# Output products as three float16 terms on 64x64 tiles, y in two float16 parts, and the dynamic convolution in far and near parts

## The reference

```python
xn = group_norm(x, 32 groups)
f = relu(Wc @ xn + bc)                          # 64 channels
gk1 = relu(mean(xn) @ Wc.T + bc)                # pixel mean
g_kern = gk1 * Wkk + bkk                        # 3x3 per channel
sk = relu(Wc @ max over 16x16 blocks of xn + bc)  # 3x3 per channel
dynW = relu(Wck[:, 0] * g_kern + Wck[:, 1] * sk + bck)   # 64x64x3x3 of each image
y = conv3x3(f, dynW) + b_ad
out = x + Wf @ y + bf                           # back to 256 channels
```

## Time and profile before

| what | us |
|---|---|
| median of three timed runs | 511.08 |
| lowest and highest of them | 510.58, 513.79 |
| span of the profiled execution, first to last instruction | 507.5 |
| median less span | 3.6 |
| PE busy in the span | 487.8 (96%) |
| ACT, DVE, POOL busy | 426.6, 418.9, 296.2 |
| DMA, mean rate over the span | 311 GB/s |

### The profile page before, as it was taken

The page is one execution under the profiler, slowest core; times in us unless marked ns, Lnnn a source line. Parts: engine busy times, 40 slices in busy tenths (PEclk is TensorE's granted clock), DMA queues, the critical chain, the costliest instruction groups (busy, mean ns, idle before and its releaser), DMA issues.

```text
span 507.5 us, 19231 instructions
## 1 busy us (share of the span) xinstructions
PE 487.8 (96%) x8349; PEld 383.7 (76%) x8349; DVE 418.9 (83%) x653; ACT 426.6 (84%) x486; POOL 296.2 (58%) x231
## 2 busy tenths in 40 slices
PE   5989999999999999999999999999999999999993
PEld 2454664677788888888888978888887878888781
DVE  6978879988888889888888988888889887888544
ACT  5779999998999999999999899999999989995231
POOL 5224586555577655556775555577655556765543
PEclk9999999999999999999999999999999999999997
DMA  8945778999898998998999999989999998953467
GB/s 335 418 134 201 265 283 289 366 353 349 323 333 334 323 332 340 348 359 293 320 362 333 333 365 343 318 297 360 307 366 334 341 333 298 361 208 145 185 270 296
DMA packets 48868, 158.01 MB, mean 311 GB/s; under 512 B 4752, under 2 KB 15888, under 8 KB 48784
## 3 DMA queue, kind: packets, MB, share of 16 engines
q1 hardware_dynamic: 34096, 93.07, 54.0%
q10 hardware_dynamic: 14688, 63.70, 31.0%
HBM read 75.94 MB, written 75.50 MB: 298 GB/s over the span
## 4 chain that ended last, share of the span: by engine, by line
PE 81%; ACT 2%; DVE 0%; issue 0%; DVEq 0%; ACTq 0%
PE ps L1129 30%; PE ps L1260 23%; PE ps L1228 21%; PE ps L1179 7%; ACT unused L609 1%; DVE X L859 0%; ACT unused L596 0%; ACT f_hi L688 0%; DVEq L153 0%; ACT f L694 0%; ACT Y L586 0%; PE ps L1372 0%; ACT dyn_b L709 0%; ACT dyn_hi L707 0%; ACTq L130 0%
## 5 line engine op out<-in xcount | busy, mean ns | idle before, releaser
L859 DVE SCALAR_TENSOR_TENSOR X<-ps,out_bias,X 128x960 f32<-128x960 f32 (+1 forms) x189 | 185.2, 1008 | 17.1 <-PE ps L1260 16.8
L1260 PE MATMUL ps<-Y,const 64*64 64x480 f32 (+1 forms) x1536 | 165.1, 486 | 0.0
L596 ACT ACTIVATE unused<-X,neg_mean 128x2304 bf16<-128x2304 f32 x60 | 132.0, 2201 | 0.4 <-DVE neg_mean L998 0.4
L512 POOL TENSOR_TENSOR dyn_a<-const,pool_g 128x576 f32<-128x576 f32 x30 | 34.9, 1165 | 163.8 <-DVE pool_g L883 163.8
L609 ACT ACTIVATE unused<-X 128x2304 bf16<-128x2304 f32 x60 | 126.9, 2115 | 0.0
L1228 PE MATMUL ps<-X,wcn_t 64*64 64x384 f32 (+1 forms) x1296 | 115.5, 486 | 0.7 <-issue 0.7
L935 DVE TENSOR_REDUCE feats<-X 128x6 f32<-128x1536 f32 x64 | 111.6, 1744 | 0.0
L1228 PEld LDWEIGHTS ps<-X,wcn_t 64*64 64x64 f32 x1296 | 82.0, 133 | 29.8 <-issue 7.4
L1260 PEld LDWEIGHTS ps<-Y,const 64*64 64x64 f32 x1536 | 78.2, 133 | 7.5 <-issue 2.8
L527 POOL TENSOR_TENSOR f_lo<-f,f_hi 128x1152 f16<-128x1152 f32 x32 | 71.4, 2232 | 19.5 <-ACT f L694 19.5
L1129 PE MATMUL ps<-f_hi,dyn_hi 64*64 64x480 f16 x1152 | 69.0, 365 | 2.5 <-ACT dyn_hi L715 1.1
(11 more groups left out here) (101 smaller groups left out, 541.8 us busy)
## 6 DMA issues: line engine op xcount, KB each, us to landing
X<-x SPq DMA_DIRECT2D x63, 1152.0 KB, 9.5
out<-X ACTq DMA_DIRECT2D x54, 1152.0 KB, 9.7
out<-X SPq DMA_DIRECT2D x7, 1152.0 KB, 8.0
out<-X SPq DMA_DIRECT2D x6, 480.0 KB, 3.5
stack<-f_hi SPq DMA_DIRECT2D x64, 32.5 KB, 2.5
stack<-f_lo SPq DMA_DIRECT2D x64, 32.5 KB, 5.4
X<-x SPq DMA_DIRECT2D x2, 576.0 KB, 7.1
upper<-f_hi SPq DMA_DIRECT2D x32, 32.5 KB, 3.5
```

Of the source, the lines that this page charges most:

```text
L596: nc.scalar.activation(unused[:, t], pixels(u, t), ACT.Square, scale=1.0 / SIDE, bias=neg_mean[:, n % 2, 1:2], accum_out=feats[:, (n + 1) ...
L859: nc.vector.scalar_tensor_tensor(out=out, in0=unit_psum(piece, bank, col), scalar=out_bias[:, t:t + 1], in1=out, op0=ALU.add, op1=ALU.add) ...
L1260: mm = nc.tensor.matmul(ps[rows, bank + q, col:col + width], wft[lanes, t, rows], Y[lanes, n % 2, at:at + width], start=True, stop=True)
```

## The change

- Output units: wft is scaled by a power of two and split into float16 parts wf_hi and wf_lo (wf_small is wf_hi over 4096). y is split into Y_hi and Y_lo (float16). Each unit is now three products in place of one float32 product. There are four units of 336 columns and two of the near part; the near units run as `products_near`, 12 groups of 4 matmuls of 240 columns, whose row tiles exchange the PSUM bank halfway. Y_hi and Y_lo have one buffer each.
- Convolution: in place of main and rest, a far part (7 rows of each tile, 336 columns) and a near part (5 rows, 240 columns), each with three terms of 9 groups of 4 matmuls. The near part reads one row across the middle of the image, which SP copies (four copies of 64x52 elements for each image in place of five of 64x260). `stack`, `upper` and `conv_rest` are gone.
- y leaves PSUM in four instructions: ACT writes Y_hi of the far part and of the near part (`y_high_out`), DVE writes Y_lo of each (`y_low_out`).
- Output bias: `channel_mean` on ACT now adds it to x in place while it sums (for images 0 and 1 POOL does it, `add_bias`). DVE's maxima wait for that.
- ACT no longer makes the relu of the dynamic weights; POOL does, with two-operation TENSOR_SCALARs (min with a large number, then max with 0). POOL's first product is now TENSOR_SCALAR on a stored per_gain, and POOL also makes the Newton factor. ACT takes over f_bias and mean_act from DVE.
- The projection is cut 512, 512 and 128 (+11) columns, with a new order of turns. Squares are now taken of image i+3. SP issues all stores.
- New orders on every engine, and new orders for the first four and last two images.

Core of the diff (lines left out are marked):

```diff
-CONV_BANKS = (0, 1)
-REST_BANK = 6
+ROWS = (7, 5)
+PART = tuple(rows * SIDE for rows in ROWS)
+FIRST = (((0, 7), (10, 17)), ((14, 19), (0, 5)))
+CHUNKS = ((0, 512), (512, 512), (1024, 128))
+PIECES = ((0, PART[FAR]), (PART[FAR], PART[FAR]), (2 * PART[FAR], PART[NEAR]))
+UNIT_BANKS = (2, 6, 6, 6, 2, 6)
+PENULT_AIDED = (5,)
+LAST_AIDED = (1, 3)
...
-        sp.dma_start(stack[lanes, n % 2, 0:some, :], f[0:CM, n % 2, HROWS + 1 - some:HROWS + 1, :]) \
-            .then_inc(stacked[u], 16)
-        sp.dma_start(stack[lanes, n % 2, some:STACK_ROWS, :], f[CM:P, n % 2, 1:1 + some, :]) \
-            .then_inc(stacked[u], 16)
-        if part == 0:
-            sp.dma_start(upper[CM:P, n % 2], f[0:CM, n % 2, HROWS + 1 - some:HROWS + 1, :]) \
-                .then_inc(stacked[u], 16)
+        sp.dma_start(f[CM:P, n % 2, 0:1, :], f[0:CM, n % 2, HROWS:HROWS + 1, :]) \
+            .then_inc(arrived[n % 2], 16)
+        sp.dma_start(f[0:CM, n % 2, HROWS + 1:HROWS + 2, :], f[CM:P, n % 2, 1:2, :]) \
+            .then_inc(arrived[n % 2], 16)
...
+for i in range(1, N - 1):
+    load(i + AHEAD, 0)
+    seam_low(i)
+    load(i + AHEAD, 1)
+    seam_high(i + 1)
+    store(i - 1, 0)
+    store(i - 1, 1)
...
-    nc.gpsimd.tensor_tensor(dyn_a[:], w0, g, ALU.mult).then_inc(dyn_step, 1)
-    nc.gpsimd.tensor_tensor(dyn_b[:], w1, s, ALU.mult).then_inc(dyn_step, 1)
-    pool.wait_ge(dyn_step, count(m, 2, DYN_STEPS))
-    nc.gpsimd.tensor_tensor(dyn_a[:], dyn_a[:], dyn_b[:], ALU.add).then_inc(dyn_step, 1)
-    pool.wait_ge(dyn_step, count(m, 3, DYN_STEPS))
-    nc.gpsimd.tensor_tensor(dyn_a[:], dyn_a[:], b0, ALU.add).then_inc(dyn_step, 1)
+    nc.gpsimd.tensor_scalar(dyn_a[:], per_gain[:], mean_act[:, n % 2, MEAN:MEAN + 1], 1.0,
+                            ALU.mult, ALU.mult).then_inc(dyn_step, 1)
+    nc.gpsimd.tensor_tensor(dyn_b[:], w1, s, ALU.mult).then_inc(dyn_step, 1)
+    pool.wait_ge(dyn_step, count(m, 1, SUM_STEPS))
+    nc.gpsimd.tensor_tensor(dyn_a[:], dyn_a[:], beside[:], ALU.add).then_inc(dyn_step, 1)
+    pool.wait_ge(dyn_step, count(m, 3, SUM_STEPS))
+    nc.gpsimd.tensor_tensor(dyn_a[:], dyn_a[:], dyn_b[:], ALU.add).then_inc(dyn_step, 1)
+        pool.wait_ge(dyn_step, count(n - SUMS, SUM_STEPS, SUM_STEPS))
+        pool.wait_ge(conv_mm[NEAR], count(n, -1))
+        nc.gpsimd.tensor_scalar(dyn_hi[:, n % 2], dyn_a[:], MOST, 0.0, ALU.min, ALU.max) \
+            .then_inc(dyn_hi_ready, 1)
+def weights_relu(n):
+    if inside(n):
+        nc.gpsimd.tensor_scalar(dyn_b[:], dyn_a[:], MOST, 0.0, ALU.min, ALU.max).then_inc(dyn_relu, 1)
...
+        nc.gpsimd.tensor_scalar(e, var, r0, r0, ALU.mult, ALU.mult).then_inc(newton_step, 1)
+        pool.wait_ge(newton_step, count(m, 1, NEWTON_STEPS))
+        nc.gpsimd.tensor_scalar(by, e, -0.5, 1.5, ALU.mult, ALU.add).then_inc(newton_step, 1)
+        pool.wait_ge(newton_step, count(m, 2, NEWTON_STEPS))
+        wait(pool, f_mm, n, -len(CHUNKS), len(CHUNKS))
+        nc.gpsimd.tensor_scalar(wcn_t[:, n % 2], wct[:], r0, by, ALU.mult, ALU.mult) \
+            .then_inc(wcn_ready, 1)
...
+def add_bias(n):
+    pool.wait_ge(bias_known, HALVES)
+    pool.wait_ge(f_mm, count(n, len(CHUNKS), len(CHUNKS)))
+    pool.wait_ge(maxima, count(n, 2 * HALVES, 2 * HALVES))
+    pool.wait_ge(squares, halves_done(n, 1))
+    for t in range(HALVES):
+        nc.gpsimd.tensor_scalar(pixels(n, t), pixels(n, t), 1.0, out_bias[:, t:t + 1], ALU.mult, ALU.add) \
+            .then_inc(biased, 1)
...
+for n in range(EARLY, N):
+    weight_sums(n)
+    weights_high(n)
+    if n == EARLY:
+        f_low(n)
+    projection(n + 1)
+    weights_relu(n)
+    weights_low(n)
+    scale_mean(n + 2)
+    if n > EARLY:
...
-        nc.scalar.activation(Y[:, n % 2, 0:2 * MAIN].rearrange("p (b f) -> p b f", b=2),
-                             ps[:, 0:2, 0:MAIN], ACT.Identity).then_inc(y_main, 1)
+        nc.scalar.activation(part_y(Y_hi, part), part_psum(part), ACT.Identity, scale=1.0 / Y_SCALE) \
+            .then_inc(y_high[part], 1)
-        nc.scalar.activation(unused[:, t], pixels(u, t), ACT.Identity, scale=1.0 / PIX,
-                             accum_out=feats[:, n % 2, t, MEAN:MEAN + 1]).then_inc(means, 1)
+        nc.scalar.activation(pixels(u, t), pixels(u, t), ACT.Identity, bias=out_bias[:, t:t + 1],
+                             accum_out=feats[:, n % 2, t, SUM:SUM + 1]).then_inc(means, 1)
-        nc.scalar.activation(dyn_hi[:, n % 2], dyn_a[:], ACT.Relu).then_inc(dyn_hi_ready, 1)
-        if n not in POOL_RELU:
-            nc.scalar.activation(dyn_b[:], dyn_a[:], ACT.Relu).then_inc(dyn_relu, 1)
+        nc.scalar.activation(f_bias[:, n % 2:n % 2 + 1], proj[:, NEG:NEG + 1], ACT.Identity, scale=-1.0,
+                             bias=bcs[:])
+        nc.scalar.activation(mean_act[:, n % 2], proj[:, 0:TAPS + 1], ACT.Relu, scale=-1.0, bias=bcs[:]) \
+            .then_inc(relu_ready, 1)
...
+for i in range(TURN + 1, N):
+    y_high_out(i - 1, NEAR)
+    features(i + 1)
+    channel_mean(0, i + 3)
+    channel_mean(1, i + 3)
+    f_out(i + 1)
+    square_sum(0, i + 3)
+    y_high_out(i, FAR)
+    square_sum(1, i + 3)
+    deviation(i + 2)
...
-        nc.vector.tensor_reduce(Y[:, n % 2, 2 * MAIN:HPIX], both, AX.X, ALU.add).then_inc(y_rest, 1)
+        nc.vector.scalar_tensor_tensor(out=part_y(Y_lo, part), in0=part_y(Y_hi, part), scalar=-Y_SCALE,
+                                       in1=part_psum(part), op0=ALU.mult, op1=ALU.add) \
+            .then_inc(y_low[part], 1)
...
+        for q, h in ((0, 0), (1, 1), (0, 1), (1, 0)):
+            lanes = slice(CM * q, CM * (q + 1))
+            r = FIRST[part][q][h] + dy
+            bank, at = (q, 0) if part == FAR else (NEAR_BANK + q, NEAR_AT)
+            mm = nc.tensor.matmul(
+                ps[CM * h:CM * (h + 1), bank, at:at + PART[part]],
+                w[lanes, n % 2, tap, :],
+                f[lanes, n % 2, r:r + ROWS[part], LEFT - 1 + dx:LEFT - 1 + dx + SIDE],
+                start=(term == 0 and tap == 0), stop=(term == order[-1] and tap == TAPS - 1))
+    turns = ((0, 0, 0), (1, 1, 0), (0, 0, 1), (1, 1, 1), (0, 2, 0), (1, 0, 0), (0, 2, 1), (0, 1, 0),
+             (1, 0, 1), (0, 1, 1), (1, 2, 0), (1, 2, 1))
+    leaves = {(0, 0): 1, (0, 2): 2, (1, 1): 1}
+    enters = {(1, 0): 1, (0, 1): 1, (1, 2): 2}
+    turned = n - TURN - 2
+    for q, c, t in turns:
+        at, width = CHUNKS[c]
+        if c == len(CHUNKS) - 1:
+            width += FEATS
+        for h in ((0, 1), (1, 0))[q]:
+            if t == 0 and (q, c) in enters:
+                pe.wait_ge(f_handed[1 - q][h], count(turned, enters[q, c], 1 + q))
+            lanes = slice(CM * q, CM * (q + 1))
+            src = half(n % RING, t) + HPAD * h + at
...
-        mm = nc.tensor.matmul(ps[rows, bank + q, col:col + width], wft[lanes, t, rows],
-                              Y[lanes, n % 2, at:at + width],
-                              start=True, stop=True)
+terms = ((wf_hi, Y_hi), (wf_small, Y_lo), (wf_lo, Y_hi))
+    for s, (w, y) in enumerate(terms):
+        for q, h in ((0, 0), (1, 1), (0, 1), (1, 0)):
+            lanes, rows = (slice(CM * tile, CM * (tile + 1)) for tile in (q, h))
+            mm = nc.tensor.matmul(ps[rows, bank + q, 0:width], w[lanes, t, rows], y[lanes, at:at + width],
+                                  start=(s == 0), stop=(s == len(terms) - 1))
+    mm.then_inc(out_mm, 1)
+                    side = (turn + q) % 2
+                    if turn == 1 and s == 0:
+                        pe.wait_ge(handed[1 - q], count(n, 2 * (k - 4) + 2, 4))
+                    mm = nc.tensor.matmul(ps[rows, bank + side, q * width:(q + 1) * width], w[lanes, t, rows],
+                                          y[lanes, at + side * width:at + (side + 1) * width],
+                                          start=(s == 0), stop=(s == len(terms) - 1))
+                    if turn == 0 and s == len(terms) - 1:
+                        mm.then_inc(handed[q], 1)
+            if turn == 1:
+                mm.then_inc(out_mm, 1)
...
+    elif i > EARLY:
+        conv(i, FAR, 0)
+        unit(1, i - 1)
+        project_f(i + 1)
+        unit(2, i - 1)
+        conv(i, FAR, 1)
+        group_sums(i + 2)
+        unit(3, i - 1)
+        conv(i, FAR, 2)
+    units_near(i - 1)
+    for term in range(3):
+        conv(i, NEAR, term)
+    unit(0, i)
```

1109 lines of the change are left out of this document (556 added, 553 removed).

## The result

The changed kernel takes 547.07 us (median of 4 runs, 545.04 to 548.12) where the kernel before, on the same chip, takes 510.85. The ratio is 1.070, 95% interval 1.066 to 1.075: slower by 7%, against a forecast of 496.5 us and a range of 485 to 506. The profiled execution has a span of 545.8 us. Where some executions of a kernel were over 1.5% slower than its fastest (one of h4 took 619.85 us), medians and ratios are of the others.

The account below looks back on a forecast made before the run. PE was taken as the bound, at 14.62 us an image; chains through DVE and ACT make it 14.15. Steady part -12.6 and end -1.8 give 493.1 of span, plus 3.6: about 496.5 us, range 485 to 506.

Parts of the forecast that it names:

- 27 x 14.15 + 1.6: Images 4 to 31: 27 images of 14.15 us plus 1.6 us of irregular stalls carried over, 383.7 against 396.3 us.
- POOL's min with max: Rival, chance 0.06: two-operation form on POOL has its own price; slower than before from 1.85 us each, about 543 at 2.2.
- weight loads in series: Rival on PE, chance 0.02: 364 loads at 47 ns each need 17 us an image, about 575 us.
- starves somewhere I haven't seen: Rival, chance 0.06: the changed order starves somewhere, such as a load behind the stores; within 1% of now.
- PE's terms: PE's work per image: far term 1.30, near term 0.94, far unit 0.43, near units 1.25, projection 3.90; sum 13.69 us.
- the handover: In the projection, row tile 1 enters chunk 0 directly behind tile 0: between 0 and 0.42 us, taken as 0.2.
- The stall ahead of the projection: PE waits for DVE's y_low of the near part, queued behind unit 0: 0.26 us, making 13.95 an image.
- An image: One steady image: 13.95 us with the stall and 0.2 for the handover, 14.15 against 14.62 before.
- the largest unknown: POOL's work per image, 11.8 us, with two-operation TENSOR_SCALARs of 576 elements at 0.82 us (bounds 0.82 and 1.65).
- Both rivals on POOL's price: POOL's relus cost 1.65 us (500 to 507 us, chance 0.16), or min with max dearer still (chance 0.06).
- The start: Images 0 to 3: no change, 0 with 3 us either way.
- The end: From the first term of image 31 to the end: 20.8 us against 22.6, a gain of 1.8.

Follow-up runs that it names:

- h4: Kernel before with three 480-column output units as three float16 products, POOL splitting Y, ACT's copy to Y ahead of its second relu: 0.991 to 1.000 of the kernel before.
- g2: Changed kernel with whole-image stores, and loads from image 7 on, cut to an eighth of the pixels, all computing kept: 512.2 us.
- h6: Kernel before with whole-image stores, and loads from image 7 on, cut to an eighth of the pixels: 507.6 us, kernel before 512.2 on that chip.
- e3: Kernel before with each 480-column matmul of the convolution's main terms issued as two of 240, 370 pairs an image in place of 262: 596.1 us.
- h2: Kernel of e3 with whole-image stores, and loads from image 7 on, cut to an eighth of the pixels: 513.5 us.
- h5: Kernel of h4 with whole-image stores, and loads from image 7 on, cut to an eighth of the pixels: 494.5 us.
- e4: Kernel before with the stores that ACT issues moved to SP, at the same places of the image: 513.0 us, 0.3% slower.

## Why the prediction was wrong

**The step that failed** is the one in the steady sum that reads "27 x 14.15 + 1.6": the 1.6 us of irregular stalls were carried over from the kernel before unchanged, without a name. They are late fetches of instructions (two stops at the grid in the kernel before, 2.1 us in all, 1.51 of it at 416.6). The prediction had counted the pairs, 262 to 364 an image, but used the count only for the weight loads (23 ns a pair, right) and never asked how the instructions reach PE. In a main term of the kernel before a pair takes 51 ns (36 in 1.84 us), so 125 pairs last 6.4 us, and with the rest's short ones among them still 5.0 at the least; in the near part of the changed kernel a pair takes 27 ns (156 in 4.23 us), so they last 3.4. With DMA nearly idle (g2) a fetch starts about 0.7 us after PE has entered the block before (median), takes 1.1, and PE can go on 1.2 to 1.6 us after that: some 3.2 us, just under 3.4. Behind data transfers the start comes later, after 2.6 us in the median in the changed kernel and 3.0 in the kernel before, and after up to 6.9 and 6.5. A block of 6.4 us covers nearly all of that, one of 3.4 hardly any. That the request is made on entering a block is my reading of the starts; the traces show the packet, not the request. Of the rivals, the two slower ones (POOL's min with max, weight loads in series) had the sign and not the mechanism; the last, "starves somewhere I haven't seen", came nearest, with 6% and the wrong price.

By its own numbers, point by point:
- *PE's terms.* Far term 1.31 (1.30 foretold), near term 0.94 (0.94), far unit 0.42 (0.43), projection 4.01 (3.90 and 0.2 for the handover): right, the handover with 0.11 at about half of what I had taken. The near units took 1.42 in place of 1.25: their groups follow at 0.10 to 0.12 as summed, but 0.26 lie between the last group (501.49) and the near term (501.75). Four instructions that wait for semaphores stand there in PE's list, 0.1 us apart; I had put them at nothing.
- *The stall ahead of the projection*, 0.26 foretold for Y_lo of the near part: 0.25 (492.32 to 492.57). The number is right, by two errors that cancel. DVE took the unit 0.25 us after PE had ended it, where 0.42 was taken, so Y_lo ended at 492.31, level with PE's columns and not 0.22 behind them. But from there to PE's next start it was 0.25, where the sum had 0.04 for a semaphore.
- *An image*, 14.15 foretold: 14.39 undisturbed, and 14.43 in g2. Of the 0.24 the near units are 0.17; the third far term took 1.46 (498.87 to 500.33) in place of 1.30, another 0.16, and the projection gives 0.09 back.
- *POOL*, the largest unknown. The groups by form give 741 and 667 ns for the two-operation forms of 576 elements, under the 0.82 taken. Both rivals on POOL's price are out (the first names two relus but counts three operations at 1.65), and so are weight loads in series. The Trainium skill's rule ("GPSIMD Engine Reference", section "Elementwise — side-by-side cycle accounting") that one or two operations cost the same loop was the better guide than the row of 1.65 us.

```profile
L506 POOL TENSOR_SCALAR dyn_a<-per_gain,mean_act 128x576 f32<-128x576 f32 x30 | 22.2, 741 | 55.5 <-ACT mean_act L716 55.5
L525 POOL TENSOR_SCALAR dyn_b<-dyn_a 128x576 f32<-128x576 f32 x30 | 20.0, 667 | 2.2
```

- *The start*, put at "0, with 3 us either way": +13.6, and still +8.5 in g2 (its image 4 at 97.08). The timeline of the changed kernel names the waits:

```profile
27.23 1.50 PE L1220 MATMUL ps<-f_hi,dyn_hi 64*64 64x336 f16 x36 [1.80 <-ACT dyn_hi L746]
...
41.40 0.49 PE L1306 MATMUL ps<-Y_hi,wf_hi 64*64 64x336 f16 x4 [2.91 <-ACT f L733]
...
42.22 2.04 PE L1220 MATMUL ps<-f_hi,dyn_hi 64*64 64x240 f16 x36
```

The products for bias and scale stand ahead of the first projection now, and the first term starts 3.8 us later than before (23.42). The first unit shares banks with the projection of the next image and waits 2.91 for ACT to empty them; behind that idle time the clock is down (0.50 granted), and a near term takes 1.80 (42.22 to 44.02) in place of 0.94. Between 20 and 100 us g2 has 6.8 us at the lower level, the changed kernel 13.6, the kernel before none. I had read the order of these instructions and not priced it. No run tested this part alone; that these waits make up the 8.5 is argued.
- *The end*, 20.8 foretold: 26.5, but 21.4 in g2. The step was right, and the rest is one stop of 1.73 us and stores that come late.

Put together: 493.1 foretold for the span, 508.0 measured without traffic (start 8.5, images 5.9, end 0.6: the sum of what was mis-sized), and 37.8 more with the traffic, 27.5 of them between image 4 and image 31, where the stops at the grid sum to 28. So even without late fetches the change would have been worth nothing: g2 stands at 1.005 of the kernel before, and the kernel before under the same cut (h6) at 0.991.

## What to carry to other kernels

Count instructions, not only columns: a change that makes matmuls shorter shortens the time in which a block of instructions is used up, and where DMA is busy too, PE runs dry at places where the program has no wait (label "issue", inside a run of equal matmuls, an instruction packet beside it). Where such stops are frequent, look at the granted clock behind them too. Split such a suspicion with two runs, one that takes the traffic away from the dense kernel and one that takes it from the other; either alone misleads. And a stall that is carried over into a forecast needs a name first: here 1.6 us that looked like noise were the only trace of what decided.

## What the runs showed of the hardware

- PE's instructions come in packets of 16 KB, one for 256 entries of its list (here some 125 pairs of load and matmul), over the DMA engines that move the data: where traffic is full, 16 data packets are in flight before a fetch starts and 15 beside it (medians over the stops of e3). A packet takes 0.88 to 1.49 us on one engine in the changed kernel, and PE goes on 1.2 to 1.6 us after it has landed. With little traffic no stop of this kind is left, in four kernels (g2, h2, h5, h6).
- The cost is far from linear. In the kernel before, 36 more pairs an image cost 17 to 18 us, 108 more 85 us, of which up to 20 go with the lower clock behind the stops; with DMA nearly idle 108 more cost 6 to 8 us (h2 against h6, by spans and by ratios), of which nearly 4 are columns (27 groups at 4.5 ns in 31 images).
- How the same bytes are moved counts once the program is dense: with stores spread over the image 620 us, from ACT's queue 577 and 605, back to back on SP 547. At 262 pairs, moving the stores from ACT to SP changed the time by some 2 us (e4).
- Transfers of 32 partitions reached some 255 GB/s with DMA busy all the time, those of 128 partitions 412.
